# A norm's small statistics (seven instructions on 128x8 numbers) on GpSimd in place of VectorE

## What is computed

```python
x = L0_attn_x                       # (4, 1024, 128)
xn = _layernorm(x)
s = _L0_attn_ref(xn, ...)           # 6 layers, each:
    xn = _layernorm(x, ln1_w[i], ln1_b[i])
    q, k, v = xn @ wq[i], xn @ wk[i], xn @ wv[i]     # 8 heads of 16
    q = softmax(q, axis=-1); k = softmax(k, axis=-2)
    x = (q @ (k^T @ v)) @ wo[i] + bo[i] + x
    xn = _layernorm(x, ln2_w[i], ln2_b[i])
    hdn = xn @ w1[i]; hdn = where(hdn >= 0, hdn, 0.01 * hdn)
    x = hdn @ w2[i] + x
g = _silu(_L0_ffn_ref(xn, ...))     # top-1 of 8 experts
x = x + s * g
```

## Time and profile before

| | us |
|---|---|
| median of three executions | 635.31 (633.61 to 637.16) |
| the profiled execution: its time | 636.8 |
| its span, first to last instruction | 635.1 |
| TensorE busy | 601.5 (95%) |
| VectorE busy | 527.4 (83%) |
| ScalarE busy | 455.5 (72%) |
| GpSimd busy | 297.6 (47%) |

### The profile page before, as it was taken

One profiled execution on the slowest core, in us unless ns is written; L12 is line 12 of the kernel. 1 busy time (PEld: TensorE's weight loads), 2 busy tenths in 40 slices (PEclk: granted clock), 3 DMA queues, 4 the chain that ended last, 5 costly groups with the idle time before them and its releaser, 6 DMA issues.

```text
span 635.1 us, 12769 instructions
## 1 busy us (share of the span) xinstructions
PE 601.5 (95%) x4230; PEld 537.2 (85%) x4230; DVE 527.4 (83%) x1375; ACT 455.5 (72%) x813; POOL 297.6 (47%) x279
## 2 busy tenths in 40 slices
PE   8699769999999999999999999999999999999985
PEld 8588759879888998998988988988988898898875
DVE  5715678998998898998898999898898889887664
ACT  2635647867877876886886887887787787786671
POOL 4511244666777233243243343243376666775342
PEclk9967698999999999999999999999999999999998
DMA  8931214224326443543533534533332532431103
GB/s 279 326 126 67 101 33 151 68 96 162 97 67 188 133 123 102 168 131 104 184 114 107 174 119 124 163 116 115 134 99 64 162 122 80 125 126 59 34 8 125
DMA packets 62308, 77.41 MB, mean 122 GB/s; under 512 B 6946, under 2 KB 52002, under 8 KB 62243
## 3 DMA queue, kind: packets, MB, share of 16 engines
q1 hardware_dynamic: 59760, 72.37, 35.4%
q0 software_dynamic: 2048, 4.20, 2.4%
q10 hardware_dynamic: 434, 0.02, 0.1%
HBM read 41.97 MB, written 34.60 MB: 121 GB/s over the span
## 4 chain that ended last, share of the span: by engine, by line
PE 67%; DMA 10%; DVE 9%; ACT 5%; issue 4%; SPq 3%; POOL 2%; ACTq 0%; DVEq 0%; POOLq 0%
PE psY L450 19%; PE psS L488 6%; PE psT L460 6%; PE psM L470 6%; PE psT L348 5%; PE psT L519 5%; PE psH L353 5%; PE psH L354 5%; PE psH L355 5%; DMA through<-blocks 5%; DMA turned<-through 4%; DVE st L774 3%; SPq L303 2%; ACT xnT L675 2%; DVE blocks L1043 1%
## 5 line engine op out<-in xcount | busy, mean ns | idle before, releaser
L450 PE MATMUL psY<-w_all,hid 128*128 128x128 f32 x1536 | 190.2, 276 | 0.9 <-DVE X L982 0.9
L450 PEld LDWEIGHTS psY<-w_all,hid 128*128 128x128 f32 x1536 | 183.3, 193 | 3.8 <-issue 1.3
L1004 DVE TENSOR_TENSOR hid<-psH,hsl 128x512 f32<-128x512 f32 x192 | 122.3, 675 | 29.2 <-ACT hsl L637 29.0
L1216 POOL TENSOR_TENSOR rstd<-veps,minus_half 128x8 f32<-128x8 f32 x52 | 85.8, 1650 | 115.2 <-DVE veps L791 115.2
L637 ACT ACTIVATE hsl<-psH 128x512 f32<-128x512 f32 x192 | 109.2, 591 | 23.0 <-PE psH L355 21.9
L1265 POOL TENSOR_TENSOR xn_lo<-xn,xn_hi 128x512 fp32r<-128x512 f32 x48 | 61.1, 1274 | 72.7 <-ACT xn_hi L693 72.7
L353 PE MATMUL psH<-xn_hi,w_hi 128*128 128x512 f32 x192 | 85.7, 446 | 6.4 <-DVE hid L1004 5.5
L1287 POOL TENSOR_TENSOR qsm<-qe,qrec 128x1024 f32<-128x1024 f32 x24 | 46.5, 1936 | 90.0 <-DVE qrec L1083 90.0
L659 ACT ACTIVATE xh<-X,shift,rstd 128x128 f32<-128x128 f32 x192 | 78.8, 483 | 10.0 <-POOL shift L1219 9.9
L774 DVE BATCH_NORM_STATS2 st<-X 128x6 f32<-128x128 f32 x384 | 78.8, 279 | 0.8
L354 PE MATMUL psH<-xn_hi,w_lo 128*128 128x512 f32 x192 | 76.0, 396 | 0.0
(11 more groups left out here) (140 smaller groups left out, 1024.8 us busy)
## 6 DMA issues: line engine op xcount, KB each, us to landing
through<-blocks SPq DMA_DIRECT2D x23, 512.0 KB
turned<-through SPq DMA_DIRECT2D x92, 128.0 KB, 2.8
through<-turn SPq DMA_DIRECT2D x23, 512.0 KB, 2.8
turn<-through SPq DMA_DIRECT2D x92, 128.0 KB, 2.9
wb<-expert_rows SPq DMA_DIRECT2D x40, 128.0 KB, 2.1
w_all<-in_w_dram SPq DMA_DIRECT2D x12, 256.0 KB, 5.1
sorted_x<-blocks SPq DMA_DIRECT2D x5, 512.0 KB, 5.8
xs<-sorted_x SPq DMA_DIRECT2D x10, 256.0 KB, 3.1
```

The lines of the kernel that those rows point to most:

```text
L450: last = nc.tensor.matmul(tile(psY, t), tile(hid[:, c, :], t), w2_all[:, n // NBATCH, c, :], start=(c == 0 and t == 0), stop=(c == NC - 1) ...
L1004: nc.vector.tensor_tensor(hid[:, i % NC, :], psH[:, i % 2, :], hsl[:, i % 2, :], ALU.max) \
L1216: nc.gpsimd.tensor_tensor(rstd[:, norm, :], veps[:, norm, :], minus_half[:, :], ALU.pow) \
```

## The change

The seven small instructions move from VectorE's `token_statistics` into GpSimd's `reciprocal_deviations`, which now waits for `st` itself. Line 791 scaled and added in one instruction; GpSimd does it without the scaling, so factors are moved: `negmean` and `sdev` are scaled by two and four, `veps` is a plain sum, four times what it was, and one more instruction doubles `rstd` at the end. So a pair of ln1 and ln2 has 14 VectorE instructions fewer, and each norm has ten GpSimd instructions in place of two. Waits that stood in front of VectorE's small statistics stand in front of the `bn_stats` now (`ln2_shift`, `ln1_shift` of the norm before), and `variances1` is gone from VectorE's slot.

```diff
-            def token_statistics(norm, name, st_count, count):
-                dve.wait_ge(sig(name + "_st"), st_count)
-                nc.vector.tensor_tensor(negmean[:, norm, :], st[:, norm, :, 1], st[:, norm, :, 4], ALU.add)
-                nc.vector.tensor_tensor(sdiff[:, norm, :], st[:, norm, :, 1], st[:, norm, :, 4], ALU.subtract)
-                nc.vector.tensor_tensor(sdev[:, norm, :], st[:, norm, :, 2], st[:, norm, :, 5], ALU.add) \
-                    .then_inc(sig(name + "_sum"), 1)
-                dve.wait_ge(sig(name + "_sum"), count)
-                nc.vector.tensor_tensor(sdiff[:, norm, :], sdiff[:, norm, :], sdiff[:, norm, :], ALU.mult)
-                nc.vector.tensor_scalar(negmean[:, norm, :], negmean[:, norm, :], -0.5, None, ALU.mult)
-                nc.vector.tensor_scalar(sdev[:, norm, :], sdev[:, norm, :], 1.0 / D, EPS, ALU.mult, ALU.add) \
-                    .then_inc(sig(name + "_sq"), 1)
-                dve.wait_ge(sig(name + "_sq"), count)
-                nc.vector.scalar_tensor_tensor(veps[:, norm, :], sdiff[:, norm, :], 0.25, sdev[:, norm, :],
-                                               ALU.mult, ALU.add).then_inc(sig(name + "_var"), 1)
...
                     dve.wait_ge(sig("x1_added"), n + 1)
+                    wait(dve, "ln2_shift", n)
                     tile_statistics(1, "ln2", lambda t: xb(X, n % NBATCH, t * P, P))
-                    wait(dve, "ln2_shift", n)
-                    token_statistics(1, "ln2", n + 1, n + 1)
...
-            def variances1(n):
-                if there(n) and n > 0:
-                    dve.wait_ge(sig("ln1_shift"), n)
-                    token_statistics(0, "ln1", 2 * n + 2, n + 1)
...
-            def reciprocal_deviations(norm, name, count):
-
+            def reciprocal_deviations(norm, name, st_count, count):
+                pool.wait_ge(sig(name + "_st"), st_count)
+                nc.gpsimd.tensor_tensor(negmean[:, norm, :], st[:, norm, :, 1], st[:, norm, :, 4], ALU.add)
+                nc.gpsimd.tensor_tensor(sdiff[:, norm, :], st[:, norm, :, 1], st[:, norm, :, 4], ALU.subtract)
+                nc.gpsimd.tensor_tensor(sdev[:, norm, :], st[:, norm, :, 2], st[:, norm, :, 5], ALU.add) \
+                    .then_inc(sig(name + "_sum"), 1)
+                pool.wait_ge(sig(name + "_sum"), count)
+                nc.gpsimd.tensor_tensor(sdiff[:, norm, :], sdiff[:, norm, :], sdiff[:, norm, :], ALU.mult)
+                nc.gpsimd.tensor_scalar(negmean[:, norm, :], negmean[:, norm, :], -1.0, None, ALU.mult)
+                nc.gpsimd.tensor_scalar(sdev[:, norm, :], sdev[:, norm, :], 4.0 / D, 4.0 * EPS, ALU.mult, ALU.add) \
+                    .then_inc(sig(name + "_sq"), 1)
+                pool.wait_ge(sig(name + "_sq"), count)
+                nc.gpsimd.tensor_tensor(veps[:, norm, :], sdiff[:, norm, :], sdev[:, norm, :], ALU.add) \
+                    .then_inc(sig(name + "_var"), 1)
                 pool.wait_ge(sig(name + "_var"), count)
-                nc.gpsimd.tensor_tensor(rstd[:, norm, :], veps[:, norm, :], minus_half[:, :], ALU.pow) \
+                nc.gpsimd.tensor_tensor(veps[:, norm, :], veps[:, norm, :], minus_half[:, :], ALU.pow) \
                     .then_inc(sig(name + "_rstd"), 1)
                 pool.wait_ge(sig(name + "_rstd"), count)
-                nc.gpsimd.tensor_tensor(shift[:, norm, :], negmean[:, norm, :], rstd[:, norm, :], ALU.mult) \
+                nc.gpsimd.tensor_tensor(shift[:, norm, :], negmean[:, norm, :], veps[:, norm, :], ALU.mult)
+                nc.gpsimd.tensor_scalar(rstd[:, norm, :], veps[:, norm, :], 2.0, None, ALU.mult) \
                     .then_inc(sig(name + "_shift"), 1)
```

More of the change, by code:

```diff
@@ L775, in tile_statistics @@
                 last.then_inc(sig(name + "_st"), 1)
-            def token_statistics(norm, name, st_count, count):
-                dve.wait_ge(sig(name + "_st"), st_count)
-                nc.vector.tensor_tensor(negmean[:, norm, :], st[:, norm, :, 1], st[:, norm, :, 4], ALU.add)
-                nc.vector.tensor_tensor(sdiff[:, norm, :], st[:, norm, :, 1], st[:, norm, :, 4], ALU.subtract)
-                nc.vector.tensor_tensor(sdev[:, norm, :], st[:, norm, :, 2], st[:, norm, :, 5], ALU.add) \
-                    .then_inc(sig(name + "_sum"), 1)
-                dve.wait_ge(sig(name + "_sum"), count)
-                nc.vector.tensor_tensor(sdiff[:, norm, :], sdiff[:, norm, :], sdiff[:, norm, :], ALU.mult)
-                nc.vector.tensor_scalar(negmean[:, norm, :], negmean[:, norm, :], -0.5, None, ALU.mult)
-                nc.vector.tensor_scalar(sdev[:, norm, :], sdev[:, norm, :], 1.0 / D, EPS, ALU.mult, ALU.add) \
-                    .then_inc(sig(name + "_sq"), 1)
-                dve.wait_ge(sig(name + "_sq"), count)
-                nc.vector.scalar_tensor_tensor(veps[:, norm, :], sdiff[:, norm, :], 0.25, sdev[:, norm, :],
-                                               ALU.mult, ALU.add).then_inc(sig(name + "_var"), 1)
             def input_statistics(b, half):
                 tile_statistics(2 + b % 2, "in", lambda t: xb(xraw, b, t * P, P), range(4 * half, 4 * half + 4))
-            def input_variances(b):
-                wait(dve, "x0_ready", b - 1)
-                token_statistics(2 + b % 2, "in", 2 * b + 2, b + 1)
             def route():
@@ L942, in _ @@
             norm1_half(0, 0)
-            token_statistics(0, "ln1", 2, 1)
             dve.wait_ge(sig("x_loaded_1"), 16)
@@ L946, in _ @@
             input_statistics(1, 1)
-            input_variances(1)
             dve.wait_ge(sig("ln1_shift"), 1)
@@ L956, in _ @@
             input_statistics(2, 1)
-            input_variances(2)
             dve.wait_ge(sig("x0_ready"), 2)
@@ L1026, in statistics1 @@
                         dve.wait_ge(sig("x0_ready"), n + 1)
+                    wait(dve, "ln1_shift", n)
                     wait(dve, "y_added", 2 * (n - NBATCH) + half + 1)
                     norm1_half(n % NBATCH, half)
-            def variances1(n):
-                if there(n) and n > 0:
-                    dve.wait_ge(sig("ln1_shift"), n)
-                    token_statistics(0, "ln1", 2 * n + 2, n + 1)
             def blocks_of_norm1(n):
@@ L1147, in slot @@
                 key_maxima(s - 1)
-                variances1(s)
                 query_maxima(s - 1)
@@ L1271, in deviations2 @@
                     wait(pool, "xh2_ready", 4 * n)
-                    reciprocal_deviations(1, "ln2", n + 1)
+                    reciprocal_deviations(1, "ln2", n + 1, n + 1)
             def deviations1(n):
@@ L1279, in deviations1 @@
                         pool.wait_ge(sig("xh1_first_ready"), 1)
-                    reciprocal_deviations(0, "ln1", n + 1)
+                    reciprocal_deviations(0, "ln1", 2 * n + 2, n + 1)
             def scale_queries(n):
@@ L1319, in slot @@
                     weigh(1)
-            reciprocal_deviations(2, "in", 1)
-            reciprocal_deviations(0, "ln1", 1)
-            reciprocal_deviations(3, "in", 2)
-            reciprocal_deviations(2, "in", 3)
+            reciprocal_deviations(2, "in", 2, 1)
+            reciprocal_deviations(0, "ln1", 2, 1)
+            reciprocal_deviations(3, "in", 4, 2)
+            pool.wait_ge(sig("x0_ready"), 1)
+            reciprocal_deviations(2, "in", 6, 3)
             keep_normalised(0)
             keep_normalised(1)
-            reciprocal_deviations(3, "in", 4)
+            pool.wait_ge(sig("x0_ready"), 2)
+            reciprocal_deviations(3, "in", 8, 4)
             slots(slot)
```

2 lines of the change are left out of this document (removed).

## The result

The changed kernel takes **643.02 us** in the median of four runs (638.08 to 643.56), the kernel before 635.18 beside it: ratio 1.010, 95% interval 1.0061 to 1.0139. It is slower by 1.0%, 4.8 us over the 638.2 forecast and at the very end of the range, 643. The profiled execution took 643.56 us with a span of 641.8, against 636.8 and 635.1 before: 6.7 us more.

What follows compares the result with a forecast made beforehand. TensorE was taken to bound the middle; +2.9 (middle slots) +1.2 (slots 2, 25) +0.6 (prologue) -1.2 -0.6 (VectorE's relief) gave +2.9 us, 639.7 for the profiled execution and 638.2 for the median; range 634.4 to 643 us.

Steps and rivals of the forecast that it cites:

- the sum for the longest norm it allowed: Whole kernel with each norm 0.85 us longer: +5.5 us, and three more slots with 0.2 each at most, 641.4 us.
- What bounds the kernel: Middle, 110 to 560 us: TensorE sets the time; VectorE's work counts only where TensorE waits for it.
- the room in each slot: Middle slots, before `expk`: 0.09 us spare in five, 0.44 in two; ten others hide about 1 us.
- The cost of a norm on GpSimd: Each norm's chain to `shift`: 0.65 us later worked out, 0.6 taken, bounds 0.16 and 0.85.
- Where it is paid: Middle: five slots waiting for `shift` pay 2.55 us, two more 0.3, the other 13 hide it; +2.9.
- Slots 2 and 25: Outside the middle window, ScalarE waits for `shift` there with TensorE behind it: +0.6 us each, +1.2.
- The prologue: Start: input 1's norm queues on GpSimd behind ln1, its tiles 2.2 us later, `qmax` at 27.8: +0.6 us.
- What VectorE's relief gives: Slot 3: `expk` earlier, -1.2 us; slot 4: `mix` in time, -0.6; elsewhere freed VectorE time brings nothing.
- The signs that were named: Trace values that would show the forecast: norm duration, waits for `shift`, `expk` and `xnT`, VectorE's busy time, slot 3's `expk`.
- second rival: Norms on GpSimd: small instructions cost twice VectorE's, norm 2.1 us later, some 669 us; chance 0.13, mostly near 645 or below.
- GpSimd's `qsm`: Third rival, eight slots with indirect DMAs: GpSimd's queue makes `qsm` late by 0.1 us, 642 to 643 us; chance 0.05.
- first rival: DMA loop: VectorE's relief makes `blocks` earlier and removes TensorE's 2.2 us of `xnT` waits, 632.2 us; chance 0.07.

Runs made afterwards that it cites:

- bare delay of 0.85 us: Kernel before plus three unused, mutually waiting small GpSimd multiplications ahead of ln2's power, statistics still on VectorE: 651.02 us, ratio 1.0147.
- norm 2 alone: Kernel before with only the seven small statistics of the second norms (ln2) moved to GpSimd: 642.04 us against 636.35, ratio 1.0094.
- norm 1 alone: Kernel before with only the small statistics of the first norms (ln1, from item 1 on) moved to GpSimd: 633.72 us, ratio 0.995.

## Why the prediction was right in kind and short in size

The measured time lies at the end of the range by some luck: the sum for the longest norm it allowed ended at 641.4, and the range reached 643 for two rivals that didn't come.

**What bounds the kernel: right.** The loss is TensorE waiting for `expk` behind ScalarE behind the norm, in slots with no shelter, and the slots with expert products hide it, as the room in each slot had said. The bare delay of 0.85 us shows that length alone is enough for it.

**The cost of a norm on GpSimd: mis-sized, 0.65 worked out and 0.6 taken, 0.87 measured.** The step that failed is the spacing of 0.16 us, taken from a pair of two-input instructions for all ten. Behind the first `tensor_scalar` the next instruction starts 0.30 us later (160.28 to 160.58); the waits for itself, 0.28 from start to start with the instruction, were right. The seven took 1.65 us instead of 1.48, and the last two 0.41 instead of 0.36. The upper bound, 0.85, was about the truth; the discount for one-input instructions went the wrong way.

**Where it is paid: right, at the wrong length.** "5 x (0.60 - 0.09)" and two slots more, +2.9, became +4.6. At the measured length the same sum gives 5 x 0.78 + 2 x 0.43 = 4.8, and with "three more slots with 0.2 each at most" 5.4 at most; measured were 3.1 + 1.8 = 4.9, less the 0.4 that the expert slots gave back. The five slots that took 0.66 to 0.78 us longer (4, 6, 8, 19, 23) answer to the five at 0.78. So the slots were counted well, and the length was the error. The prediction's own number for this case, +5.5 to 6.1 in all, lies within 1.2 us of the 6.7.

**Slots 2 and 25: +1.2 forecast.** From slot 24 to the end of the kernel the changed one lost 1.3 us, where 0.6 was forecast for slot 25 alone. In slot 2 TensorE's wait for `expk` rose from 1.7 us to 3.6; what of that the slot cost can't be told, since it lies where the clock differs between executions.

**The prologue: mis-sized.** Input 1's tiles began at 20.57 instead of 17.45, 3.1 later where 2.2 was worked out, and with them `qmax`, at 30.40 instead of 27.20 where 27.8 was forecast: the queue of norms on GpSimd was the mechanism named, and longer. Alone the prologue's move costs 1.7 to 2.2 us instead of 0.6.

**What VectorE's relief gives: wrong in its size and its place.** -1.2 was forecast in slot 3 and -0.6 in slot 4. In slot 3 `expk` did come earlier against the slot's addition to X, by 0.2 us and not 1.2 (94.46 - 83.58 = 10.88 in the changed kernel; before, `expk` at 93.08 and the addition at 82.01, 11.07). The relief itself was worked out well: `hid`, behind the small statistics, started 6.23 us behind the addition (89.81) where it was 7.59 (89.60), 1.36 earlier. Then `pad_run`, the instruction above that fell into an `xn_lo`, took 1.27 us instead of 0.17, ahead of `negkmax`, for which `expk` waits, and 1.10 of the 1.36 was gone. What the prediction lacked was this collision; it is read from the rows, no run took it away by itself. TensorE's wait for `expk` grew from 2.33 to 3.50 us, because it came there sooner: its wait for `hid` fell from 2.7 to 0.3, and from addition to addition the slot took 26.20 us instead of 26.97, 0.8 less. The wait for `mix` stayed, once 0.6 us. On the other hand, norm 1's move brought 0.5%, where the sum had nothing outside slots 3 and 4.

**The signs that were named.** The seven in 1.3 to 1.5 us: 1.65. ScalarE's wait some 6 us or more in over 8 slots: 17.5 in 19, most of it in slots that hide it. TensorE's waits for `expk` some 3 us in 5 to 7 slots: 3.7 in 8. VectorE's busy time down by 45 us: 35.4, or 0.68 a norm, since the 0.90 of the chain holds gaps and overlaps with what stands around it. TensorE's share in the middle over 98.5%: 98.7.

**The rivals.** The twofold price (second rival) didn't come: 0.20 to 0.24 us per instruction. GpSimd's `qsm` was not late: between 108 and 580 us TensorE's loads waited for it once, 0.3 us; ahead of that, TensorE waited 0.9 us for it between 76 and 80 us. The first rival, relief that reaches the DMA loop, is real but small and belongs to norm 1: TensorE's waits for `xnT` fell from 2.2 to 1.3 us in the changed kernel and 1.2 with norm 1 alone (2.3 with norm 2 alone). In the whole change it is covered by norm 2's loss.

## What to carry to other kernels

Ask of each piece of a small chain whether anyone waits for its end. The same seven instructions cost 0.9% on a slower engine where a tight chain runs through them (norm 2) and gave 0.5% where the time was to spare (norm 1); moving both hid the one behind the other. A chain that is just covered has no linear price: a first 0.85 us cost 1.5% on the second chip, and the next, on top of the change, 3.3%; so shorten such a chain before moving it. Price a run of tiny instructions by their starts, each kind apart, not by their durations. And when an edit shifts work in time, look at which small instructions of VectorE's now start inside a long one of GpSimd's: one such case ate the relief of slot 3.

## What the runs showed of the hardware that was not expected

- **A lock between VectorE and GpSimd.** VectorE's small instructions on SBUF that started inside a GpSimd `xn_lo` (1.27 us) ended 0.02 to 0.04 us behind it (a second one right behind it, some 0.1): 1.24 us in place of 0.17. The power on 128x8 (1.67 us) held none of them, and `xn_lo` didn't hold the `bn_stats` (eight in 1.65 us at 155.88, beside an `xn_lo` from 155.69 to 156.96). An edit that moved one such instruction by some tenths of a us cost 8 of them a us each.
- **Tiny instructions on GpSimd** (128x8): 0.20 to 0.24 us each, the next one 0.17 us behind the start of a `tensor_tensor`, 0.30 behind the start of the first `tensor_scalar`, 0.28 across a wait for itself. VectorE has 0.17 us, and 0.08 to 0.09 from start to start.
- **Chips differ by as much as the change brings.** The kernel before took 636.4, 641.9 and 644.8 us on three chips. In the traces of the two slower ones VectorE's addition starts up to 1.5 us later behind TensorE's L519, mostly by 1.0 to 1.5 in five to seven slots, all of them behind indirect DMAs; the sum is of the size of the difference. The ratio of the same change was 1.010 in one measurement and 1.0143 in another, with intervals that meet.
- **TensorE's clock in the first 108 us.** Between 30 and 40 us the granted clock was 0.53 in the kernel before and 0.76 in the changed one, and between 50 and 108 us 0.81, 0.80, and 0.69 in the kernel with only the prologue moved: stretches at the lower level of 1.2 GHz lie elsewhere in each execution. From the first to the last run of a kernel the time varies by up to 7 us. That last kernel's profiled execution took 641.2 us against its median of 638.5.
